# A decoder layer's side stages cut into smaller pieces, its weight quantisation put behind the norms, and one copy moved ahead of a norm

## What is computed

```python
q, k, v = (x @ W).reshape(B, T, H, D) for W in (Wq, Wk, Wv)
q, k = rmsnorm(q, q_rms_w), rmsnorm(k, k_rms_w)
scores = einsum('bthd,bshd->bhts', q, k) / sqrt(D) - dist * slope      # causal
y = rmsnorm(softmax(scores) @ v, subln_w)
x = layernorm(x + y.reshape(B, T, H * D) @ Wproj)

query, key = ctx @ Wq.T + bq, ctx @ Wk.T + bk
x = layernorm(x + x @ softmax(query @ key.T))

def quant_weight(w): s = mean(abs(w)) + EPS; return clip(round(w / s), -1, 1) * s
def quant_act(x): s = max(max(abs(x), -1), EPS) / 127; return clip(round(x / s), -128, 127) * s
h = sigmoid(quant_act(x) @ quant_weight(w_gate).T) * (quant_act(x) @ quant_weight(w_up).T)
x = layernorm(x + quant_act(h) @ quant_weight(w_down).T)
```

## Time and profile before

| | us |
|---|---|
| median of 3 executions | 468.44 (467.79 to 471.14) |
| the profiled execution | 471.42 |
| its span, first to last instruction | 469.6 |

### The profile page before, as it was taken

One profiled execution on the slowest core, in us unless ns is written; L12 is line 12 of the kernel. 1 busy time (PEld: TensorE's weight loads), 2 busy tenths in 40 slices (PEclk: granted clock), 3 DMA queues, 4 the chain that ended last, 5 costly groups with the idle time before them and its releaser, 6 DMA issues.

```text
span 469.6 us, 9764 instructions
## 1 busy us (share of the span) xinstructions
PE 413.1 (88%) x2740; PEld 366.7 (78%) x2740; DVE 316.3 (67%) x984; ACT 307.8 (66%) x1217; POOL 233.6 (50%) x380
## 2 busy tenths in 40 slices
PE   4999879988999899988999899979998999977652
PEld 3898779978898779877998899869996898863331
DVE  2367666677767776777667776685677666656984
ACT  4788866777767775776668767758487757612441
POOL 4565454455545554555666645655465643332102
PEclk9999989999999999999999999998999999985885
DMA  7951101111211111111102101111110000000000
GB/s 207 356 176 36 34 19 61 36 35 35 80 35 35 36 35 34 36 35 35 35 3 67 36 1 34 36 34 36 34 58 1 13 1 1 12 2 0 0 13 34
DMA packets 34916, 21.20 MB, mean 45 GB/s; under 512 B 2608, under 2 KB 34608, under 8 KB 34864
## 3 DMA queue, kind: packets, MB, share of 16 engines
q1 hardware_dynamic: 34048, 20.20, 14.4%
q10 hardware_dynamic: 816, 0.39, 0.3%
HBM read 19.53 MB, written 1.05 MB: 44 GB/s over the span
## 4 chain that ended last, share of the span: by engine, by line
issue 32%; POOL 30%; PE 19%; DVE 10%; ACT 6%; DMA 1%; POOLq 0%; ACTq 0%; DVEq 0%
POOL qk_rstd L429 13%; POOL w_lo L393 9%; PE ps L641 5%; POOL y_rstd L454 4%; PE ps L497 3%; POOL bias L444 2%; PE ps L596 1%; PE ps L620 1%; PE ps L608 1%; ACT sq L827 1%; PE ps L682 1%; PE ps L665 1%; DVE qk_n L1057 1%; DMA w_raw<-in_L_attn_Wv 1%; DVE pT L1096 1%
## 5 line engine op out<-in xcount | busy, mean ns | idle before, releaser
L429 POOL TENSOR_TENSOR qk_rstd<-qk_sum,minus_half 128x2 f32<-128x2 f32 x128 | 89.8, 701 | 57.1 <-ACT sq L827 57.0
L641 PE MATMUL ps<-w_hi,xT_hi 128*128 128x384 f32 x256 | 100.7, 393 | 2.4 <-DVE w_lo L913 2.0
L454 POOL TENSOR_TENSOR y_rstd<-y_sum,minus_half 128x2 f32<-128x2 f32 x64 | 44.3, 692 | 111.9 <-DVE y_sum L1079 111.9
L827 ACT ACTIVATE sq<-ps 128x130 f32<-128x130 f32 x256 | 71.2, 294 | 35.7 <-PE ps L641 35.6
L641 PE MATMUL ps<-w_hi,xT_lo 128*128 128x384 f32 x256 | 87.6, 342 | 0.0
L641 PE MATMUL ps<-w_lo,xT_hi 128*128 128x384 f32 x256 | 87.6, 342 | 0.0
L393 POOL TENSOR_TENSOR w_lo<-w_raw,w_hi 128x256 fp32r<-128x256 f32 x93 | 68.9, 742 | 3.8 <-ACT w_hi L754 3.8
L838 ACT ACTIVATE prob<-score,neg_max 128x128 f32<-128x128 f32 x64 | 26.0, 406 | 67.5 <-DVE neg_max L1104 67.5
L1057 DVE TENSOR_TENSOR qk_n<-ps,qk_rstd 128x256 f32<-128x256 f32 x128 | 53.5, 418 | 19.9 <-POOL qk_rstd L429 19.0
L827 ACT ACTIVATION_READ_ACCUMULATOR sq<-ps 128x1 f32 x256 | 55.7, 219 | 0.0
L641 PEld LDWEIGHTS ps<-w_hi,xT_hi 128*128 128x128 f32 x256 | 49.3, 192 | 6.4 <-issue 4.0
(11 more groups left out here) (170 smaller groups left out, 1025.0 us busy)
## 6 DMA issues: line engine op xcount, KB each, us to landing
w_raw<-in_L_attn_Wq SPq DMA_DIRECT2D x31, 128.0 KB, 2.2
w_raw<-in_L_attn_Wk SPq DMA_DIRECT2D x31, 128.0 KB, 2.3
w_raw<-in_L_attn_Wv SPq DMA_DIRECT2D x31, 128.0 KB, 2.4
wp_raw<-in_L_attn_Wproj SPq DMA_DIRECT2D x4, 512.0 KB, 5.5
x_sb<-in_x SPq DMA_DIRECT2D x4, 256.0 KB, 4.8
ff_raw<-in_L_ffn_w_gate SPq DMA_DIRECT2D x1, 1024.0 KB, 8.5
ff_raw<-in_L_ffn_w_up SPq DMA_DIRECT2D x1, 1024.0 KB, 7.8
ff_raw<-in_L_ffn_w_down SPq DMA_DIRECT2D x1, 1024.0 KB, 9.9
```

What stands on the lines that cost most here:

```text
L429: pool.tensor_tensor(qk_rstd[:, t, :], qk_sum[:, t, :], minus_half[:], ALU.pow).then_inc(s_rs[t], 1)
L454: pool.tensor_tensor(y_rstd[:], y_sum[:], minus_half[:], ALU.pow).then_inc(s_ry, 1)
L641: last = pe.matmul(ps_qkv[:, t], xa[:, k, tok], wa[:, g % 3, k * 3 * D:(k + 1) * 3 * D], start=(i == 0), stop=(i == len(parts) - 1))
L827: last = act.activation(sq[:, t, a, :], ps_cols[:, t, a, :], ACT.Square, accum_out=qk_sum[:, t, a:a + 1])
```

## The change

1. **Weight quantisation.** fquant(k) moves from slot 0 to slot 1 of step 12+k, so on VectorE from between `norm(n, 0)` and `scores(n-1)` to behind `norm(n, 1)`. Its turn, fturn(k), moves to slot 1 of step 13+k.
2. **pT's copy.** In VectorE's order, `copy_pT(n-2)` stands ahead of `norm_y(n-3)`.
3. **Weight sums.** Each engine sums pieces of 512 columns instead of 1,024: six stages in slot 1 of steps 5 to 10 instead of three in steps 6 to 8; wtotal moves from step 9 to 11.
4. **Side stages of the FFN.** xm and dn are split from their moments (m1, m2), x2b into the scales (x2b) and the quantisation (x2c); ha stands directly behind u0. The planner has a room for VectorE and ScalarE that depends on the slot and on whether the step is a quad step (outside quad steps, VectorE 80 in slot 0 and 130 in slot 1), lets a unit take several joined stages in one slot, and replaces "the next unit's stages only once the one before has begun g0" by a table AFTER. gate_up_scale gets two places, in turn, as units overlap more.
5. **The end.** The plan now runs into (65, 0): VectorE's code behind the loop gets two calls of side_work.

Where the two plans put the stages (read off plan() slot by slot; number = unit):

| slot | before | after |
|---|---|---|
| (42, 0) | hb0 xm1 | hs0 t1.1 |
| (42, 1) | hs0 x2a1 | ra0 xm1 m1.1 |
| (43, 0) | ra0 x2b1 | rb0 x2a1 x2b1 x2c1 |
| (48, 0) | hb1 xm2 | hs1 t1.2 |
| (48, 1) | hs1 x2a2 | ra1 xm2 m1.2 |
| (49, 0) | ra1 x2b2 | rb1 x2a2 |
| (49, 1) | rb1 t2.2 | hq1 x2b2 |
| (55, 0) | hs2 x2a3 | hs2 t1.3 |
| (55, 1) | ra2 x2b3 | ra2 xm3 m1.3 |
| (63, 0) | th3 | rb3 |
| (63, 1) | dn3 | hq3 |
| (64, 0) | fin3 | th3 |
| (64, 1) | | dn3 m2.3 |
| (65, 0) | | fin3 |

```diff
-LOAD = dict(st0=(34, 0), x1=(16, 0), t1=(0, 17), xm=(59, 0), x2a=(44, 0), x2b=(59, 0), t2=(0, 16),
...
+LOAD = dict(st0=(52, 0), x1=(25, 0), t1=(0, 27), xm=(37, 0), m1=(55, 0), x2a=(65, 0), x2b=(50, 0), x2c=(60, 0),
...
+ROOM = ((80, 120), (130, 120)), ((200, 160), (200, 160))
+
+AFTER = dict(g0=(1, "u1"), u0=(1, "hq"), x2b=(1, "x2c"), xm=(1, "x2a"), t2=(1, "u1"), x2a=(2, "dn"))
@@ plan
-    for i in range(3):
-        put(6 + i, 1, "wsum", i)
-    put(9, 1, "wtotal", 0)
+    for i in range(6):
+        put(5 + i, 1, "wsum", i)
+    put(11, 1, "wtotal", 0)
...
-        put(12 + k, 0, "fquant", k)
-        put(12 + k, 1, "fturn", k)
+        put(12 + k, 1, "fquant", k)
+        put(13 + k, 1, "fturn", k)
...
-        psum, loads = quad and slot % 2 == 0, [38 if quad and slot % 2 else 0, 0]
+        psum, room = quad and slot % 2 == 0 or slot == 2 * 36 + 1, list(ROOM[quad][slot % 2])
...
-            if stage in IN_PSUM and psum or any(a and a + b > 100 for a, b in zip(LOAD[stage], loads)):
-                continue
+            while stages and (first or stages[0] in JOINED):
...
+                if stage in IN_PSUM and psum or any(a and a > b for a, b in zip(LOAD[stage], room)):
+                    break
@@ vector, side_work
-                        dve.tensor_reduce(w_sum[:, i:i + 1], ff_raw[:, i // 2, i % 2 * F:(i % 2 + 1) * F], AX.X, ALU.add,
-                                          apply_absolute_value=True).then_inc(s_wabs, 1)
+                        dve.tensor_reduce(w_sum[:, 2 * i:2 * i + 1], ff_raw[:, i // 2, i % 2 * 2 * BANK:(i % 2 * 2 + 1) * BANK],
+                                          AX.X, ALU.add, apply_absolute_value=True).then_inc(s_wabs, 1)
...
                     elif stage == "xm":
                         dve.tensor_tensor(res[:, 0], of[:, 0:T], x1, ALU.add).then_inc(freed, 1)
-                        wait_evacuated(dve, stage, i)
+                    elif stage == "m1":
+                        wait_evacuated(dve, "xm", i)
                         moments(1, res[:, 0])
@@ vector, loop
+                if n >= 2:
+                    copy_pT(n - 2)
                 if n >= 3:
                     norm_y(n - 3)
-                if n >= 2:
-                    copy_pT(n - 2)
@@ vector, behind the loop
+            side_work(STEPS, 1)
             sum_y(STEPS - 2)
             low_y(STEPS - 3)
             copy_pT(STEPS - 1)
             norm_y(STEPS - 2)
+            side_work(STEPS + 1, 0)
             sum_y(STEPS - 1)
```

More of the change, by code:

```diff
@@ L96, in plan @@
         quad = quad_at(slot // 2) is not None
-        psum, loads = quad and slot % 2 == 0, [38 if quad and slot % 2 else 0, 0]
+        psum, room = quad and slot % 2 == 0 or slot == 2 * 36 + 1, list(ROOM[quad][slot % 2])
         for u, stages in enumerate(todo):
-            if not stages or u > 0 and "g0" in todo[u - 1] or (stages[0], slot) == ("st0", 2 * 36) and u >= TT:
-                continue
-            stage = stages[0]
-            if stage in IN_PSUM and psum or any(a and a + b > 100 for a, b in zip(LOAD[stage], loads)):
-                continue
-            psum, loads = psum or stage in IN_PSUM, [a + b for a, b in zip(LOAD[stage], loads)]
-            put(slot // 2, slot % 2, stages.pop(0), u)
+            first = True
+            while stages and (first or stages[0] in JOINED):
+                stage = stages[0]
+                back, other = AFTER.get(stage, (1, "g0" if stage == "st0" else None))
+                if u >= back and other in todo[u - back] or stage == "st0" and u == TT and slot == 2 * 36:
+                    break
+                if stage in IN_PSUM and psum or any(a and a > b for a, b in zip(LOAD[stage], room)):
+                    break
+                psum, room = psum or stage in IN_PSUM, [b - a for a, b in zip(LOAD[stage], room)]
+                put(slot // 2, slot % 2, stages.pop(0), u)
+                first = False
         slot += 1
-    assert slot <= 2 * STEPS + 2, slot
+    assert slot <= 2 * STEPS + 3, slot
     return at
@@ L200, in decoder_kernel @@
         ff_q = sb("ff_q", [P, C], BF16)
-        w_sum = sb("w_sum", [P, 6])
+        w_sum = sb("w_sum", [P, 12])
         w_total = sb("w_total", [P, 3])
@@ L221, in decoder_kernel @@
         h_most = sb("h_most", [P, 2])
-        gate_up_scale = sb("gate_up_scale", [P, 2])
+        gate_up_scale = sb("gate_up_scale", [P, 2, 2])
         round_col, table = sb("round_col", [P, 1]), sb("table", [P, 1])
@@ L550, in side_work @@
                     elif stage == "wtotal":
-                        pe.wait_ge(s_wabs, 3)
-                        pe.wait_ge(s_wabs_act, 3)
-                        last = pe.matmul(to[:, 0:6], ones[:], w_sum[:], start=True, stop=True)
+                        pe.wait_ge(s_wabs, 6)
+                        pe.wait_ge(s_wabs_act, 6)
+                        last = pe.matmul(to[:, 0:12], ones[:], w_sum[:], start=True, stop=True)
                     elif stage == "cturn":
@@ L785, in side_work @@
                     elif stage == "wsum":
-                        act.wait_ge(s_ff[(i + 3) // 2], 16)
+                        act.wait_ge(s_ff[i // 2], 16)
                         wait(act, s_wabs_act, i)
-                        act.activation(abs_w, ff_raw[:, (i + 3) // 2, (i + 3) % 2 * F:((i + 3) % 2 + 1) * F], ACT.Abs,
-                                       accum_out=w_sum[:, i + 3:i + 4]).then_inc(s_wabs_act, 1)
+                        act.activation(abs_w, ff_raw[:, i // 2, (i % 2 * 2 + 1) * BANK:(i % 2 * 2 + 2) * BANK], ACT.Abs,
+                                       accum_out=w_sum[:, 2 * i + 1:2 * i + 2]).then_inc(s_wabs_act, 1)
                     elif stage == "cturn":
@@ L1033, in side_work @@
                     elif stage == "x2b":
+                        scale_x2(i)
+                    elif stage == "x2c":
                         quantise_x2(i)
```

35 lines of the change are left out of this document (19 added, 16 removed).

## The result

The changed kernel took 445.53 us (median of 4 runs, 444.92 to 445.95), the kernel before 468.12 us beside it (4 runs, 466.11 to 471.14). The ratio is 0.949, 95% interval 0.945 to 0.953: 22.6 us less. Forecast were 455 us, in a range from 448 to 463, so the sign and most of the mechanisms were right, and the time lies outside the range. The profiled execution of after took 445.95 us, with a span of 444.1 us.

The account below looks back on a forecast made before the run. The prediction took TensorE, busy 88% of the span, as the floor. Its terms, 7.0 + 2.0 + 1.5 + 5.5 - 2.2 = 13.8 us, off 468.44 gave 454.6, rounded to 455 us; range 448 to 463.

Parts of the forecast that it names:

- the ceiling: TensorE's idle time over the listed stretches: 27.7 us, claimed as the most that reordering the other engines can give back.
- the term of the side stages: Steps 37 to 63: the new plan of the FFN's side stages saves 5.5 of 9.18 us idle time (0 to 9).
- Quantisation and swap: Steps 21 to 26 and 29 to 34: quantisation in slot 1 and pT's copy ahead of y_n save 7.0 us.
- The swap alone: Quantisation steps: pT's copy fills DVE's wait for y_rstd, but qk_n waits for qk_rstd and moves only 0.16 us.
- rival (b): Moved quantisation contends with POOL's weight split: 0.55 us in some 12 steps, 6.6 us, giving 461 us; chance 0.08.
- Steps 13 to 18: Quantisation beside the cross-attention, gap in slot 1 partly used up: 2.0 of 4.42 us idle time saved (0 to 4.4).
- Weight sums: Steps 5 to 11: half-size sums fit DVE's gap, two new pieces land in full steps; 1.5 us saved (-1 to 4.7).
- Step 49: Worst place of the old plan: 8.60 us with TensorE busy 5.25, so 3.35 of the stretch's 9.18 us.
- The drain: Behind step 63: unit 3's last stages now stand ahead of the last y_sum and y_rstd; net 2.2 us lost (1 to 4).
- Rival (a): TensorE nearly full, shortened DVE chains only become waits for it: a third of the sum, about 463 us; chance 0.18.
- Rival (c): Behind step 63 TensorE idles until its clock falls from 2.4 to 1.2 GHz: slower, some 474 us; chance 0.05.
- Rival (d): Nearly all of TensorE's idle time closes: 23 to 24 us saved, 445 us; chance 0.07.

Follow-up runs that it names:

- b_quant: Kernel before with only the weight quantisation moved to slot 1 and its turn a step later: 458.20 us, ratio 0.979.
- b_wsum: Kernel before with only the weight sums in six halves, total at step 11: 466.65 us, ratio 0.995.
- a_blind130: Changed kernel with the same small stages but VectorE's room 130 in slot 0 too, outside quad steps: 449.75 us, ratio to before 0.960.
- b_pool: Kernel before with only GpSimd's slot 0 side work put behind qk_rstd of tile 1 instead of ahead: 464.97 us, ratio 0.992.
- b_swap: Kernel before with only pT's copy put ahead of y's norm: 463.69 us, ratio 0.991.
- a_drain5: Changed kernel with the drain's early output projections moved later, timed again in more rounds: 443.50 us (6 runs), ratio to before 0.946.
- a_drain: Changed kernel with the drain's early output projections moved to a later place, first session: 444.80 us (4 runs), ratio to before 0.948.
- a_same5: Changed kernel, unaltered, timed again in the same rounds as the repeated drain edit: 446.48 us (6 runs), ratio to before 0.953.

## Why the prediction was wrong in size

**The step that failed** is the ceiling: "That is 27.7 us, and the most that any reordering of the other engines can give back", and with it the term of the side stages, "5.5 of the 9.18 us (0 to 9)". The rows gave 12.8, more than the whole idle time of the stretch: idle time fell from 9.18 to 154.11 - 152.08 = 2.03 us, which is 7.2, and the rest, 5.7, came out of rows that were counted as busy. (The 27.7 us for all stretches were not passed; the single terms were sized by their idle time, and that is where it failed.)

Steps 29 to 34 show how busy time can fall. Both traces have 201 matmuls there, and busy time fell from 30.70 to 28.69 us. One group, of before and then of after (line, tiles, count, busy us, mean ns):

```profile
L641 PE MATMUL ps<-w_hi,xT_lo 128*128 128x384 f32 x24 | 8.1, 337 | 0.0
```

```profile
L651 PE MATMUL ps<-w_hi,xT_lo 128*128 128x384 f32 x24 | 8.1, 338 | 0.0
```

Each matmul takes the same time in both, and the durations of all that start in the stretch add up to 60.97 us in either trace. What differs is how they overlap, and a piece of before's timeline in step 34 would have shown it:

```profile
215.00 0.34 PE L641 MATMUL ps<-w_hi,xT_lo 128*128 128x384 f32 x1
215.17 0.34 PE L641 MATMUL ps<-w_hi,xT_hi 128*128 128x384 f32 x1
215.35 0.33 PE L641 MATMUL ps<-w_lo,xT_hi 128*128 128x384 f32 x1
215.52 0.34 PE L641 MATMUL ps<-w_hi,xT_lo 128*128 128x384 f32 x1
216.16 0.63 PE L665 MATMUL ps<-ident,qk_n 128*128 128x128 f32 x4 [0.30 <-issue]
```

A matmul of this kind is followed by the next one 0.17 us after its start, and is counted busy for 0.34. At 215.52 the next comes 0.64 us later: 0.64 - 0.17 = 0.47 us are lost, and the row shows 0.30 of idle time. Every such break in TensorE's stream so hides another 0.17 us under the name of busy. In steps 29 to 34 the trace of before has 15 breaks with idle time, that of after 3: 12 x 0.17 = 2.0 us, which is the fall of the busy time.

In steps 37 to 63 the row of before has to be put right first. TensorE ran at a granted clock of 0.50 from 316.0 to 319.4 us, in step 50, and what that cost is counted as busy. `b_quant` has the same side stages with the clock at 1.00 throughout, and takes the same time:

```profile
224.56:391.38 166.82, 155.95 (x1082) 143.51 (x1091) 117.39 (x373) 116.70 (x477) 92.16 (x148) 1.00 0.09 25
```

It is idle for 10.87 us, in 27 breaks; after is idle for 2.03, in 15. Of the 12.7 us between the two, 8.8 are idle time, some 2.0 (12 x 0.17, an estimate) were hidden in the breaks that are gone, and 1.8 are not accounted for one by one: eight turns of unit 3 (0.42 us, from 401.24 in before) left the stretch, and pauses shorter than the overlap show no idle time at all. The idle time was a floor of what could be gained there, not a ceiling.

By the Trainium skill, Perfetto Trace Analysis, "Identifying the Most-Contended Engine", the busy share of weight loads is the better measure, as matmuls are pipelined. The runs agree: weight loads fell by 1.4 us in steps 37 to 63 (145.18 to 143.74, one per cent, with unit 3's last stages gone from the loop), and the ceiling by them, 167.0 - 145.2 = 21.8 us, holds the 12.8. The prediction cited this rule for steps 29 to 34 and did not carry it over to the largest term.

**Point by point.**

*Quantisation and swap, forecast 7.0, bounds 3 to 10: 9.0.* The working was right, and lowering its result was not. An odd-even pair was put at 9.7 to 10.1 us; steps 32 and 33 took 5.09 + 4.72 = 9.81. "8 to 10 us" followed from it, and was then lowered to 7.0 because TensorE showed only 6.0 of idle time: the same error.

*The swap alone.* Costed at 0.16 us in each quantisation step and nothing elsewhere. It is 0.04 to 0.07 there, but 4.5 to 4.7 us in all, because wherever DVE waited for y_rstd (33.2 us in before, in 63 of 64 steps) the copy now fills that wait.

*Port contention, rival (b): out.* The quantisation's three instructions in their new place (ns, least, median, most):

```profile
L1084 DVE TENSOR_SCALAR ff_round<-ff_raw,w_inv x24: 344/474/482, 83.5 to 214.4; 128x256 f32<-128x256 f32 x24
L1086 DVE TENSOR_SCALAR ff_round<-ff_round x24: 293/295/296, 83.9 to 214.8; 128x256 f32<-128x256 f32 x24
```

The instruction that the prediction feared for, the second, stayed at 0.295 us against 0.294 in the earlier trace rows; none of the 24 overlaps an instruction of POOL. The first one does meet POOL: 17 of the 24 start 0.40 to 0.41 us into a w_lo split, as at 192.12, take 0.467 to 0.482 us, and all end 0.15 us behind the end of the split; the seven that meet no split take 0.344 to 0.346. So it waits for POOL, but the wait costs 0.13 us and not 0.55. It does not simply fall into the gap: in the step shown, y_sum starts 0.13 us behind the end of its input (sqy on ACT, 192.74 + 0.38 = 193.12). It does not set the length of that step, as score later waits 0.28 us for TensorE. (There are 24 such pieces, not the 23 of the prediction.)

*Steps 13 to 18, 2.0: 2.6.* As read.

*Weight sums, 1.5: 1.8 in the median of `b_wsum`, 2.4 in the rows of the pair.* The rows owe part of it to the clock, which in before fell in step 10 (last section). The other kernels without the edit take 35.3 to 35.7 us in steps 8 to 12, before 37.30, `b_wsum` 35.22: by rows the edit is worth some 0.3 us. What makes up the rest of its 1.8 us is open.

*Side stages, 5.5: 12.8.* Step 49 was read rightly (3.35 us forecast of its room, 8.60 to 5.49 measured). The rest was put at 2 us and brought 9.7. It came from places that the prediction held to be full: steps 43 and 44, a quad pair like the one that it quoted with 14.90 of 14.90 us, went from 17.30 to 15.32. One pair was taken for all; step 43 was not full before, and is now:

```profile
267.30:276.45 9.15, 7.75 (x60) 7.17 (x59) 7.36 (x29) 4.66 (x18) 5.33 (x9) 1.00 0.15 44
```

```profile
252.49:260.04 7.55, 7.55 (x59) 7.40 (x58) 6.56 (x23) 5.18 (x19) 4.20 (x8) 1.00 0.20 55
```

Step 56 gave 2.2, steps 50 and 51 1.8, step 46 1.1. Steps 61 to 63 gave 1.6 us up to the boundary at 375.26, since unit 3's last stages left the loop; up to the first matmul of step 64 they gave 0.3. Of what brought all this the runs show the new rooms (`a_blind130`) and POOL's order (3.0 us, `b_pool`), which may overlap; how much the finer stages give by themselves stays open. The steps that became fuller (42, 48, 55, 60 and 61) lost 0.2 to 0.5 us each, as forecast in kind.

*The drain, 2.2 lost, bounds 1 to 4.* From the boundary in step 63 to the first norm of the tail the drain went from 15.7 to 19.2 us, 3.5 lost: inside the bounds, and by the chain that was named (third_sum, the last y_sum, y_n) with one more, the early projection in front of the last scores. The whole part behind step 63 shows only +1.7, as the tail of before's profiled execution was longer than in its sister kernels (67.13 us against 64.6 to 65.4 in `b_swap`, `b_quant` and `b_wsum`).

*Rival (a), TensorE nearly full (0.18): out* (a third of the sum gives 463.8, not 463), and it was the idle time again that made it look likely. *Rival (c), the clock in the drain:* did not come, the granted clock is 1.00 over the drain of after. *Rival (d), 445 us, had 0.07:* its time was met, its reason (all idle time closes) was not the one.

## What to carry to other kernels

Where the busiest engine is pipelined, its idle time in the profile is less than what its breaks cost: measure from start to start against the pitch of an unbroken run, or take the weight loads' busy time as the floor, before lowering a gain that was worked out from the cycle itself. When a cycle has been followed link by link and gives a number, trust that number over an average of the engine that seems to bound it. And side work has a place as well as a size: with the slot in front of the critical instruction kept light the same small stages took 154.1 us of the loop, and 162.6 with as much room there as in the other slot. The drain gave 6.0 us of that back, so count the whole kernel: some 4 us.

## What the runs showed of the hardware

In ten of the twelve profiled executions TensorE's granted clock fell to 0.50 (1.2 instead of 2.4 GHz) for 3.4 us early in the loop: in seven of them in step 9, from 57.6 to 58.8 us on, and in three in step 10 (before, from 66.8 us on, `a_drain` and `a_drain5`). The two profiles of the changed kernel (after, `a_same5`) have none ahead of the tail. Step 10 of `a_drain5` and of after, columns as above, the clock behind POOL:

```profile
61.30:69.90 8.60, 6.60 (x37) 6.19 (x36) 5.17 (x17) 7.37 (x31) 4.47 (x7) 0.80 0.13 35
```

```profile
60.60:67.60 7.00, 5.00 (x37) 4.66 (x36) 4.87 (x17) 7.00 (x31) 3.43 (x5) 1.00 0.01 2
```

The same 37 matmuls, with the same instructions on DVE and ACT, take 8.64 us from start to start in the one and 7.04 in the other, and TensorE is idle for 2.0 us in both: it is ACT that is busy throughout at the full clock, so even here the half clock was not hidden. In both profiles of the drain's edit (`a_drain`, `a_drain5`) step 10 took 8.64 us. Over steps 8 to 12 this comes to 1.3 us (36.07 in `a_drain5`, 34.74 in after), and where it falls decides: `a_blind130`, with the same instructions there and its half clock in step 9, takes 34.75 (step 9 8.99 us against 7.38 in after, step 10 5.42 against 7.04). A single profile can thus be off by more than a microsecond in steps that no edit touched, which is why the gain of the drain's edit is not to be seen in the spans (444.5 and 444.1 us) and is in the medians.
